# Messages: the targets' one-hots made on GpSimd and ACT instead of on the vector engine

## The reference, cut to what matters

```
tpw = h @ W_mlp4 / sqrt(64)                 # 512 weights for each edge
w1, w2, w3, w4 = split(tpw, 4)
s0, s1 = x0[sender], x1[sender]             # 128 and 128 x 3 values of the sender
p1 = w1 * s0 * y0
p2 = (w2 * s0)[:, :, None] * y1[:, None, :]
p3 = w3[:, :, None] * s1 * y0[:, None, :]
p4 = w4 * einsum('eum,em->eu', s1, y1) / sqrt(3)
msg0 = segment_sum([p1, p4], receiver)      # edges of one receiver are added
msg1 = segment_sum([p2, p3], receiver)
```

## Time and profile before

| | |
|---|---|
| median of three runs | 1942.54 us (1939.13 to 1943.98) |
| span of the profiled execution, from its first to its last instruction | 1941.4 us |
| PE busy | 1611.2 us, 83% |
| DVE busy | 958.2 us, 49% |
| ACT busy | 701.1 us, 36% |
| POOL busy | 561.3 us, 29% |
| the messages' loop, first product to last sum | 1327.2 to 1672.0 us |

### The profile page before, as it was taken

How to read it: one execution, slowest core, us unless ns; L and a number is a source line. 1 busy time by engine, 2 the same in 40 slices (tenths; PEclk the granted TensorE clock), 3 DMA queues, 4 the chain that set the end, 5 groups by cost and what they waited for, 6 DMA issues and landing times. The chain is left out here.

```text
span 1941.4 us, 31644 instructions
## 1 busy us (share of the span) xinstructions
PE 1611.2 (83%) x9860; PEld 1169.5 (60%) x9860; DVE 958.2 (49%) x1950; ACT 701.1 (36%) x1610; POOL 561.3 (29%) x638
## 2 busy tenths in 40 slices
PE   1132298889999999889999999946999999898994
PEld 0111153568888865555999999934555455654662
DVE  8200023967776657654000000065999999632233
ACT  0000032745555543345222221144555555441331
POOL 6777500020110012125000000044555555123133
PEclk6565598989999999889999999968999999998997
DMA  9600011010103030065766554075555555518985
GB/s 292 240 7 6 18 40 41 1 26 18 23 11 82 10 84 2 1 238 163 284 232 234 197 207 171 9 186 142 159 158 152 146 157 155 190 59 270 354 260 185
DMA packets 131143, 252.87 MB, mean 130 GB/s; under 512 B 35344, under 2 KB 52596, under 8 KB 126572
## 3 DMA queue, kind: packets, MB, share of 16 engines
q1 hardware_dynamic: 91692, 171.81, 26.4%
q0 software_dynamic: 39360, 79.86, 14.7%
HBM read 196.03 MB, written 55.52 MB: 130 GB/s over the span
## 5 line engine op out<-in xcount | busy, mean ns | idle before, releaser
L2065 PE MATMUL acc<-prod,ohy 128*64 128x256 f32 x1056 | 250.7, 387 | 13.7 <-issue 7.5
L2109 ACT ACTIVATE ohy<-oh,RECS 128x64 f32<-128x64 f32 x704 | 186.7, 336 | 160.3 <-PE acc L2065 128.2
L2065 PEld LDWEIGHTS acc<-prod,ohy 128*64 128x64 f32 x1056 | 138.9, 138 | 140.0 <-issue 71.5
L2042 POOL DMA_INDIRECT rows<-up_dram,idx x176 | 167.4, 951 | 151.9 <-DVE prod L2183 107.0
L417 PE MATMUL ps<-FT,Wqkv 128*128 128x512 f32 (+1 forms) x192 | 88.1, 591 | 114.3 <-issue 114.3
L2068 PE MATMUL acc<-prod,ohy 128*64 128x256 f32 x704 | 179.6, 397 | 0.0
L273 POOL DMA_INDIRECT rec_dram<-recs,pos x157 | 161.6, 1029 | 60.2 <-issue 48.9
L1819 DVE TENSOR_SCALAR FT<-y_ps,b2T 128x188 f32<-128x188 f32 x32 | 13.2, 414 | 323.3 <-PE y_ps L1768 323.3
L1756 PE MATMUL hid_ps<-FT,W 128*128 128x188 f32 x1024 | 167.7, 325 | 0.7 <-ACT FT L1793 0.7
L2183 DVE TENSOR_TENSOR prod<-w_ps,rows 128x768 f32<-128x768 f32 x176 | 166.8, 948 | 0.0
L1756 PEld LDWEIGHTS hid_ps<-FT,W 128*128 128x128 f32 x1024 | 165.2, 192 | 0.9 <-issue 0.9
(11 more groups left out here) (389 smaller groups left out, 2725.9 us busy)
## 6 DMA issues: line engine op xcount, KB each, us to landing
W<-in_L_ffn_w SPq DMA_DIRECT2D x16, 4096.0 KB, 16.2
bankW_sp<-in_L_ffn_W_sp SPq DMA_DIRECT2D x2, 4096.0 KB, 24.0
xin<-zeros SPq DMA_DIRECT2D x31, 256.0 KB
h_dram<-h3e SPq DMA_DIRECT2D x22, 256.0 KB
h<-h_dram SPq DMA_DIRECT2D x22, 256.0 KB
QF<-q_dram SPq DMA_DIRECT2D x20, 250.0 KB, 4.2
xin_sp<-zeros SPq DMA_DIRECT2D x17, 256.0 KB
xin_fq<-zeros SPq DMA_DIRECT2D x17, 256.0 KB
```

The costliest lines, as they stand in the source:

```text
L2042: pool.indirect_dma_start(out=rows[:, t, :], out_offset=None, in_=up_dram, in_offset=bass.IndirectOffsetOnAxis(ap=idx[:, par, t:t + 1], ax ...
L2065: upper = lambda m: nc.tensor.matmul(acc[0:HALFB, bank, :].rearrange("p (b c) -> p b c", c=MUL)[:, m:4:3 - m, :], ohs[:, 1 + m, :], pr[:, ...
L2109: last = nc.scalar.activation(ohy[:, t % OHY, i, :], oh[:, par, t, :], ACT.Copy, scale=RECS[:, bass.ds(BATCH * g + t, 1), 4 + i])
```

## The change

`mark` is gone from the vector engine, except for batch 0, whose one-hots it still makes with the comparison before the loop. For batch g+1, GpSimd subtracts `local_dst` from `lane` (128 x 512 in one instruction) after it has issued the eight fetches of batch g; ACT then takes the absolute value in place, and then relu(1 - value) in place, between tiles 5 and 6 of batch g. For whole numbers this is 1 where lane and receiver are the same and 0 elsewhere. Two semaphores are new: `offsets` (subtraction done) and `distances` (absolute value done). GpSimd now waits for `weighted`, in place of the vector engine.

```diff
+            MARK_AT = BATCH - 3
...
+                offsets, distances = sems_in(st)("lane_offsets", "lane_distances")
...
+                def lane_of(tiles):
+                    return lane[:].unsqueeze(1).to_broadcast([128, tiles, HALFB])
+
+                def dst_of(batch, tiles):
+                    dst = local_dst[:, bass.ds(BATCH // EPP * batch, tiles // EPP), :].rearrange("p g t -> p (g t)")
+                    return dst.unsqueeze(2).to_broadcast([128, tiles, HALFB])
...
                                 ).then_inc(arrived[t], 16)
+                            if next_size(g):
+                                pool.wait_ge(weighted, BATCH * g + BATCH)
+                                nc.gpsimd.tensor_tensor(oh[:, 1 - par, 0:next_size(g)], lane_of(next_size(g)), dst_of(g + 1, next_size(g)),
+                                                        ALU.subtract).then_inc(offsets, 1)
+
+                        pool.wait_ge(local, 1)
                         rounds(pool, gather)
...
                                 last.then_inc(weighted, 1)
+                                if t == MARK_AT and next_size(g):
+                                    ahead = oh[:, 1 - par, 0:next_size(g)]
+                                    act.wait_ge(offsets, g + 1)
+                                    nc.scalar.activation(ahead, ahead, ACT.Abs).then_inc(distances, 1)
+                                    act.wait_ge(distances, g + 1)
+                                    nc.scalar.activation(ahead, ahead, ACT.Relu, bias=ones[:, 0:1], scale=-1.0).then_inc(one_hots, 1)
...
-                                if t == 0 and next_size(g):
-
-                                    dve.wait_ge(weighted, BATCH * g + BATCH)
-                                    mark(g + 1, 1 - par, next_size(g))
                                 take_sums(n, (t - LAG) % SUMS)
```

More of the change, by code:

```diff
@@ L2128, in take_sums @@
                             nc.vector.tensor_tensor(sums, sums, acc[:, bank, :], ALU.add).then_inc(taken, 1)
[L2130 to L2135, removed]
                         nc.vector.memset(MSG[:, 0:CLEARED_BY_DVE, :], 0.0)
@@ L2161, in between @@
                                 dve.wait_ge(local, 1)
-                                mark(0, 0, BATCH)
+                                nc.vector.tensor_tensor(oh[:, 0, :], lane_of(BATCH), dst_of(0, BATCH), ALU.is_equal).then_inc(one_hots, 1)
                         mix_on_dve(dve, between)
```

## The result

The changed kernel takes 1952.21 us (median of 13 runs, 1946.65 to 1960.80), the kernel before beside it 1942.54 us (13 runs): a ratio of 1.0048, 95% interval 1.0034 to 1.0062. That is slower by some 9 us, more than the 0.3% that can be told from no change. The prediction of no change (1942.0 us, range 1935 to 1949) was wrong.

A forecast was written before the change was run, and what follows sets the result against it. PE was taken to bound the loop at 15.18 us a batch, the vector engine close behind at 14.92. All terms cost 0 except -0.5 us of catch-up, so 1942.54 - 0.5 = 1942.0 us, range 1935 to 1949.

The forecast's parts named there:

- the comparison's 12.6 us: Vector engine's loop: removing 21 comparisons frees 21 x 0.60 = 12.6 us there, with gain 0 in the steady part.
- The 0.5 us of catch-up: After the loop's second break: PE catches up faster without the comparison, counted as -0.5 us.
- the late step of 4.26 us: PE's step after the second break, in place of 3.79 us; its 0.47 us excess was tied to a batch's comparison.
- the 0.26 us of the earlier trace: Right after the second break, in a batch start with a comparison: PE was said to wait 0.26 us for a tile.
- POOL's subtraction, cost 0: 21 subtractions added on POOL, taken as 1.28 us each; POOL's batch of 13.2 us stays below 15.18, cost 0.
- the lead of the data: POOL's fetches: issued 15.2 us before need, 3.4 us from start to use, leaving over 10 us to cover lateness.
- the 1.3 of the prediction: First fetch of each batch on POOL: expected 1.3 us later than now because of the subtraction, at cost 0.
- The reserve: ACT and DVE start when PE has added tile n-4; PE needs tile 6's one-hots with 4.4 us to spare.
- these breaks are not made by its load: Two breaks in PE's pace, losing 6.57 and 2.34 us: claimed not caused by the vector engine's load.
- ACT's pair, cost 0: Two activations per batch on ACT between tiles 5 and 6: 1.5 us a batch, never reaching PE, cost 0.
- Rival A: POOL's subtraction keeps the vector engine out of SBUF: 8.8 us slower, 1951 us, up to 1978.5; chance 0.08.
- disturbances of its kind, such as longer breaks: Grouped with ACT coming too late for PE, put at 12.6 us slower, 1955 us; chance 0.04 together.

The follow-up runs named there:

- e1_neither: Changed kernel without POOL's subtraction and ACT's two activations, batch 0's one-hots reused, so no comparison in the loop; ratio to the kernel before 1.0008.
- e11_before_lag3: Kernel before with LAG = 3 in place of 2, so the vector engine adds the sum of three tiles earlier; ratio to the kernel before 0.9991.
- e3_act_only: Changed kernel without POOL's subtraction, ACT's two activations kept but writing to a spare tile; ratio to the kernel before 1.0005.
- e4_later: Changed kernel with each POOL fetch waiting for one more tile's products; ratio to the kernel before 1.0046.
- e13_spaced: Changed kernel with a POOL memset of a spare tile behind each of a batch's first five fetches; ratio to the kernel before 0.9964, repeated 0.9955.
- e5_held_fetch: Kernel before with the first two fetches of each batch held until the vector engine has done tile 2; ratio to the kernel before 1.0365.
- e15_before_spaced: Kernel before with a POOL memset of 128 x 384 behind each of a batch's first five fetches; ratio to the kernel before 0.9969.
- e9_narrow: e5_held_fetch with 128 numbers of each row fetched and used four times, in place of 512; ratio to the kernel before 1.0359.
- e6_pieces: Changed kernel with the subtraction cut into eight pieces of 128 x 64, one behind each fetch; ratio to the kernel before 0.9972.

## Why the prediction was wrong

- **PE bounds the loop; the comparison's 12.6 us are worth nothing.** Right: e1_neither, with no one-hots made in the loop at all, is as fast as before. The 0.5 us of catch-up can't be told from the scatter of the times. In the profiles the late step of 4.26 us is in e11_before_lag3 as in the kernel before, and gone in e1_neither and e3_act_only, where the comparison is gone. But I read the 0.26 us of the earlier trace rows as a wait for a tile; the row puts it down to "issue", to nothing that the profile shows.
- **POOL's subtraction, cost 0.** This is the step that failed. Its duration (1.05 us) was near, and POOL's load and the lead of the data were right: fetches later still cost nothing more (e4_later). The first fetch came 3.20 us behind the one before it against 2.71, so the shift was about 0.5 us and not the 1.3 of the prediction, as the index copy became 0.51 us shorter. But I wrote that the second fetch would be late as well "until the distance of 1.27 against 1.90 us per tile has made it up", and took that catching up as free. It is the cost: where fetches go 1.25 to 1.29 us apart, ACT and the vector engine get PE's finished tile 1.8 us late and more, 3.16 us in the batch of 1373.12, and PE's loop is 9.6 us longer. Without the catch-up the same subtraction is free (e13_spaced), and with it and no subtraction the loop gets far longer (e5_held_fetch).
- **The reserve.** I let the vector engine depend on tile n-4. It also takes tile n-2's sum (LAG), in order, ahead of its next products. So what lies between a late event and PE is under two tiles of 1.90 us. With 1.79 us of delay 0.30 us reach PE (4.09 - 3.79), with 3.16 us 1.73 (5.52 - 3.79). Why nearly the same close fetches (1.29, 1.26 and 1.42 us; 1.28 and 1.26 us) delay by the one in some batches and by the other in others is open. LAG = 3 takes the loss away.
- **The profile of before showed it.** In both breaks of the earlier trace rows fetches go 1.26 us apart: 1323.76, 1325.03 and on without a pause to 1332.70, then 1334.79 to 1338.57; and 1538.03, 1539.28, 1540.54, 1541.79, 1543.05 ahead of the second, behind which the vector engine waited 3.48 us for PE (the row below). The 6.76 us that the vector engine waited, "behind an event that the profile puts down to nothing", began there, and e15_before_spaced takes that break away. I read "these breaks are not made by its load" and did not ask what made them.

```profile
1545.32 0.69 DVE L2128 TENSOR_TENSOR MSG<-MSG,acc 128x512 f32 x1 [3.48 <-PE acc L2065]
```

- **ACT's pair, cost 0.** Right alone (e3_act_only), its durations too. Whether it adds to the loss beside the late events is not shown: the loop is 2.9 us longer than with the subtraction alone, hardly more than the 2.3 us between two profiles of the changed kernel.
- **Rival A** gave 1951 us, and 1952 was measured. Its mechanism did not take place: the vector engine's operations are 945 and 676 ns, no longer than before, and the subtraction stands beside them unhindered. The number agrees by chance. Of what I gave a chance to, only the 0.04 for "disturbances of its kind, such as longer breaks" is near what happened. The index copy's return from 0.70 to 0.19 us shows that the comparison had held it up. The Trainium skill's rule on the pair of ports that DVE and GpSimd share (SBUF — State Buffer, SBUF's two separate sides) agrees with both.

Open: why PE's finished tiles are seen late while fetches are issued back to back, and whether only PE's are. The rows show it for engines that wait for PE; no engine waited for another's event in those stretches long enough to tell. Whether the issuing on GpSimd or the packets that follow from it are the cause is open too; e9_narrow shows only that it is not their bytes. What starts the second break of the kernel before, a fetch 3.97 us behind the one before it at 1538.03, was not found.

## What to carry to other kernels

When work is put ahead of DMA issues on an engine, ask not only whether the transfers still come in time but how they then follow on each other; a queue that catches up can cost more than one that is late. Look for the same pattern in the kernel as it is: a break in the pace that no load explains is worth explaining before anything is predicted. And count reserve to the nearest event that an engine takes in order, here n-2 and not n-4.

## What the runs showed of the hardware

- Indirect fetches of 128 rows issued from GpSimd 1.25 to 1.29 us apart delay what waits for PE by 1.8 to 3.2 us (after) and more (e5_held_fetch, where the vector engine waits 3.34 us). Eight in a row at 1.44 to 1.46 us still did so, with waits of 1.93 and 1.78 us (e6_pieces); at 1.55 us (e13_spaced), and for one distance of 1.48 us in a batch (the kernel before), the pace held. A fetch's size does not matter: 64 KB as 256 KB (1.0359 and 1.0365).
- GpSimd's subtraction with both inputs read with repeats takes 1052 ns for 128 x 512, less than its plain addition of 125 x 512, and 302 ns for 128 x 64.
- Work for nothing on GpSimd, a memset of 0.44 us behind each of five fetches in eight, made the kernel before 0.31% faster (e15_before_spaced).
